# Row maxima of the attention scores from the rounded parts alone, two heads side by side in the grouped layers

## Chip, core and metric

One NeuronCore of one Trainium2 chip. The metric is the device time of one execution in microseconds (us), lower is better. The kernel before has a median of 4727.58 us over three runs (4726.94 to 4730.17).

## What is computed

Four cross-attention layers run one after the other on x (8 batches, 512 tokens, 512 channels) with one context (8 batches, 512 keys, 1024 channels). Layer 0 has 16 heads of 64 channels and a bias on four key columns; layers 1 to 3 normalise x first and have 16 query heads of 32 channels that share 4 key/value heads. Cut to what matters:

```python
# layer 0
logits = einsum('bhqd,bhkd->bhqk', x @ Wq, ctx @ Wk) * 64 ** -0.5 + col_bias
x = softmax(logits) @ (ctx @ Wv) @ Wo + bo + x
# layers 1 to 3 (n_rep = 4 query heads per key head)
xn = x * rsqrt(mean(x * x) + eps) * norm_w
scores = einsum('btgrd,bsgd->bgrts', qg, k) / sqrt(32)
x = x + softmax(scores) @ v @ wo
```

A softmax is the same whatever constant is subtracted from a row of scores before the exponential, as long as numerator and denominator use the same one. The kernel subtracts a row maximum only to keep the exponentials in range.

## The kernel before, in words

`project_context` (L42) runs twice and leaves keys and values of all layers in DRAM. `attention_layers` (L221) runs for layer 0 (no norm, d = 64, H = 2 heads in a tile of 128 channels, T = 8 tiles) and then, in one loop, for layers 1 to 3 (the grouped layers: norm, d = 32, H = 4, T = 4). The loop over `it` takes a batch of a layer: 8 rounds in layer 0, 24 in the grouped layers; inside it stand T tiles t.

Every number is split into a rounded part (hi) and a rest (lo), and a product is hi·hi + hi·lo + lo·hi. For the scores the three products are stacked along the contraction: `q_ops` holds (hi, hi, lo) and `k_ops` (hi, lo, hi) on successive groups of d partitions, `PASS` = 4d/128 matmuls per product (two in layer 0, one in the grouped layers). Partition 96 of the last pass carries minus the row maximum in `q_ops` and ones in `k_ops`, so that `scores` (L941) leaves the shifted scores in PSUM, and ScalarE takes the exponential (L699).

TensorE's order is written out by hand (L1008 to L1069). While it makes the scores of tile t (S0, S1, ... below: `scores(it, t, n)`, the product of 128 keys of two heads), it also makes the maxima of tile t + 1 (M0, M1, ...: `maxima`, L920, 128 queries by 512 keys of one head, M = 8 in layer 0 and 16 in the grouped layers), which VectorE reduces one by one (`reduce_max`, L800). M0 to M15 cycle through the PSUM banks of `MAXB` (L322), and a maximum waits until the reduction of the last user of its bank is done (L927). In a grouped tile the order before is S0 S1, M0 M1 S2, M2 S3 M3, M4 S4 M5 O0, M6 S5 M7 O1, M8 S6 M9, M10 S7 M11 O2, M12 M13, O3 M14 M15, D, the turn, P. O0 to O3 are `outputs` (L955, probabilities times values, one matmul per head in its own 32 or 64 columns of the array), D is `denominators` (L972, likewise in columns), the turn (L934) transposes the maxima, P is `project_q` (L905, 12 matmuls) for tile t + 3. In layer 0: S0, M0 S1 M1, M2 S2 M3 O0, M4 S3 M5 O1, M6 M7 O2, O3, the turn, nine matmuls of P, D, the last three of P. After the last tile of a round stands `project_out` (L983).

VectorE's order is also written out (L847 to L895). In a tile after the first one: `take_q` (L788), the rest of the reciprocals (L823) of the tile before, the reduction of M0, in layer 0 one more reciprocal and the reduction of M1, then `normalise` (L826), then the other reductions. O0 waits for `normalise` (L963), because both use one PSUM bank.

GpSimd adds up probabilities for the denominators (L593) and makes the rests (L599, L603). SyncE issues all DMAs: `load_k` (L409), `load_q` (L423, which spreads hi and lo over `q_ops`), x and results. K and Q tiles lie in rings of four (`RING`), loaded three tiles ahead (`AHEAD`). In layer 0 the x of the next round is split in two halves in tile 5 (L442, L640, L809), and P of that tile needs both.

Of the kernel before, what the change touches and what calls it, by code (L numbers as in the profile page):

```python
# [5 lines left out]
P = 128  # L6
# [214 lines left out]
def attention_layers(nc, name, kind, x_in, x_out, k_scratch, v_scratch, wq, wo, norm_w=None, bias=None):  # L221
# [41 lines left out]
    with ExitStack() as mem:  # L263
        def sb(n, shape, dt):
            return mem.enter_context(nc.sbuf_tensor(f"{name}_{n}", shape, dt))
# [105 lines left out]
        def last_use(n):  # L371

            return max(m for m in range(n) if MAXB[m] == MAXB[n])

        def k_head(h):
            return 0 if kind.shared else h

# [22 lines left out]
        def raw_chunk(c, slot):  # L400
            n = (CK if c < HALF else T) // HALF
            return w_raw[:, slot, :].rearrange("p (k n) -> p k n", k=n), range((c % HALF) * n, (c % HALF + 1) * n)

        block = mem.enter_context(nc.Block())
        X0 = P - d

        @block.sync
        def _(sp):
            def load_k(it, t, n=None):  # L409

                s = t % RING
                b, l = (0, 0) if n is None else (n % B, n // B)
                for i, part in enumerate((0, 1, 0)):
                    at = (i * d) % P
                    dst = as_f32(k_ops[at:at + d, s, :, (i * d) // P, :])
                    if kind.shared:
                        src = k_scratch[b, INNER0 // P + l, part][t * d:(t + 1) * d, :]
                        src = src.rearrange("(h p) s -> p h s", h=1)
                    else:
                        src = k_scratch[b, t, part].rearrange("(h p) s -> p h s", h=H)  # L420
                    sp.dma_start(dst, src).then_inc(k_in[s], DMA)

            def load_q(it, t):  # L423
                s = t % RING
                sp.wait_ge(q_lo, it * T + t + 1)
                for h in range(H):
                    for i, part in enumerate((qn_hi, qn_hi, qn_lo)):
                        at = (i * d) % P
                        sp.dma_start(as_f32(q_ops[at:at + d, s, h, (i * d) // P, :]),
                                     as_f32(part[h * d:(h + 1) * d, :])).then_inc(q_in[s], DMA)  # L430

            def load_v(t, n=None):
                b, l = (0, 0) if n is None else (n % B, n // B)
# [121 lines left out]
                sp.wait_ge(w_in[0], (2 * L + 2) * DMA)  # L555
                sp.wait_ge(nw_in, (L + 1) * DMA)
            for t in range(AHEAD):
                sp.wait_ge(k_in[t], ring_count(N, t) * (3 * DMA))
# [4 lines left out]
        def _(pool):  # L563
# [32 lines left out]
            def rest_q(it, t):  # L596
                if has_norm:
                    pool.wait_ge(q_hi, it * T + t + 1)
                    pool.tensor_tensor(qn_lo[:, :], qf[:, :], as_f32(qn_hi[:, :]), ALU.subtract).then_inc(q_lo, 1)  # L599

            def rest_output(it, t):
                pool.wait_ge(o_hi, it * T + t + 1)
# [21 lines left out]
        def _(act):  # L624
# [26 lines left out]
            def round_q(it, t, first=False):  # L651
                if has_norm:
                    act.wait_ge(q_taken, it * T + t + 1)
                else:
                    act.wait_ge(q_proj, it * T + t + 1)
                if not first:
                    it_p, t_p = (it, t - 1) if t > 0 else (it - 1, T - 1)
                    act.wait_ge(q_in[t_p % RING], ring_count(it_p, t_p) * (3 * H * DMA))
                if has_norm:
                    act.activation(qn_hi[:, :], qf[:, :], ACT.Copy).then_inc(q_hi, 1)  # L660
                else:
                    act.activation(qn_hi[:, :], bank(QB), ACT.Copy, scale=scale).then_inc(q_hi, 1)

            def shift(it, t):

# [62 lines left out]
        def _(dve):  # L728
# [59 lines left out]
            def take_q(it, t, first=False):  # L788
                if has_norm:
                    dve.wait_ge(q_proj, it * T + t + 1)  # L790
                    if not first:
                        dve.wait_ge(q_lo, it * T + t)
                    dve.wait_ge(inv_done, it + 1)
                    dve.tensor_tensor(qf[:, :], bank(QB), inv[:, :], ALU.mult).then_inc(q_taken, 1)
                else:
                    dve.wait_ge(q_hi, it * T + t + 1)
                    dve.scalar_tensor_tensor(out=qn_lo[:, :], in0=bank(QB), scalar=scale, in1=as_f32(qn_hi[:, :]),
                                             op0=ALU.mult, op1=ALU.subtract).then_inc(q_lo, 1)

            def reduce_max(it, t, n):  # L800
                dve.wait_ge(smax, (it * T + t) * M + n + 1)
                col = n % QT + 32 * (n // QT)
# [95 lines left out]
        def _(pe):  # L898
# [20 lines left out]

            def maxima(it, t, n):  # L920

                s = t % RING
                if n == 0:
                    pe.wait_ge(k_in[s], ring_count(it, t) * (3 * DMA))
                    pe.wait_ge(q_in[s], ring_count(it, t) * (3 * H * DMA))
                elif MAXB[n] in MAXB[:n]:
                    pe.wait_ge(reduced, (it * T + t) * M + last_use(n) + 1)  # L927
                h, q = n // QT, n % QT
# [12 lines left out]
            def scores(it, t, n):  # L941

                s, kt, hp = t % RING, n // (H // 2), n % (H // 2)
                if n == 0:
                    pe.wait_ge(shifted, it * T + t + 1)
# [62 lines left out]
            with pe.Fori(0, N) as it:  # L1008
                for t in range(T):
# [4 lines left out]
                    if t == 0 and H == 2:  # L1014
                        pe.wait_ge(added, CK + it * CK - 2)
                    for r in range(NS):
                        if has_norm and r == NS - 1:
                            outputs(it, t, KT - 1)
                        if MAXB.index(DENB) in (2 * r, 2 * r + 1):
                            pe.wait_ge(normed, 1 + it * T + t)  # L1020
                        maxima(*place(it, t + 1), 2 * r)

                        summing = has_norm and t == 0 and r == NS // 2
                        if summing:

                            pe.wait_ge(reduced, (it * T + t + 1) * M + last_use(2 * r + 1) + 1)
                            sum_squares(it + 1)
                        if t == 0 and r == 0 and H == 2:
                            pe.wait_ge(added, CK + it * CK)
                        if H // 2 + r < NS and not (r == 0 and has_norm):  # L1030
                            scores(it, t, H // 2 + r)
                        if r == 0:
                            pe.wait_ge(bank_q, it * T + t + AHEAD)
                        if not summing:
                            maxima(*place(it, t + 1), 2 * r + 1)
                        if r == 0 and has_norm:
                            scores(it, t, H // 2)
                        if r in OUT_AT and not (r == NS - 1 and has_norm):
                            outputs(it, t, OUT_AT.index(r))
                        if summing:  # L1040
                            pe.wait_ge(ms_step, MS * (it + 1) + 1)
                            maxima(*place(it, t + 1), 2 * r + 1)
                    if not has_norm:
                        outputs(it, t, KT - 1)
                    else:
# [67 lines left out]
```

## Time and profile before

| | |
|---|---|
| median of 3 runs | 4727.58 us |
| runs | 4730.17, 4727.58, 4726.94 us |
| span of the profiled execution | 4730.0 us (all but equal to the highest run, 2.4 above the median) |
| busy: PE (TensorE matmul), weight loads | 94%, 57% |
| busy: VectorE, ScalarE, GpSimd | 54%, 41%, 33% |
| stages by the span: keys, values, layer 0, grouped layers | to 580, to 1062, to 2412, to 4730 us |

A busy PE is not a PE at its peak: an entry of the profile lasts from issue to the modelled end, so neighbours overlap, and what a matmul costs in a stream is the distance between starts. The prediction reads those distances from the timeline.

### The profile page before, as it was taken

Reading aid. Unit: us, or ns where it says so; the run is one execution under the profiler, and the core shown is the slowest. Engines: PE = TensorE matmul, PEld = TensorE weight load, DVE = VectorE, ACT = ScalarE, POOL = GpSimd, SP = SyncE. Lnnn points to the kernel's source line nnn. Section 1 sums busy time; section 2 is a strip of 40 time slices with the busy share of each in tenths; the row PEclk is TensorE's granted clock in tenths of the full one; section 3 lists DMA queues with packets and bytes.
Section 4 is the critical chain, followed back from the end, with each engine's and each line's share of the span. In section 5 each row is a group of like instructions: output and inputs, shape, how many; then the busy total and the mean of one; then the engine's idle time right before and its main releaser. Section 6 shows DMA issues by size and latency. Waiting matters only on the chain. (4 is left out here: it accounts for less than half of the span.)

```text
span 4730.0 us, 63902 instructions
## 1 busy us (share of the span) xinstructions
PE 4434.4 (94%) x20450; PEld 2718.5 (57%) x20450; DVE 2572.9 (54%) x3575; ACT 1926.9 (41%) x2348; POOL 1579.5 (33%) x827
## 2 busy tenths in 40 slices
PE   7999799978999999999969999999999999999998
PEld 6888688864555655565535454445444544454454
DVE  2211200015455455544557767776777677767776
ACT  2111211113333333333326555655565555555554
POOL 0000000002444435434424444444444443444444
PEclk9999899998999999999979999999999999999999
DMA  4333422234434444444432232232222222222233
GB/s 158 127 129 133 148 83 82 80 99 120 115 100 118 115 108 111 118 107 113 113 89 71 82 88 71 75 98 83 73 74 86 84 82 75 84 85 73 75 89 95
DMA packets 301727, 461.94 MB, mean 98 GB/s; under 512 B 44954, under 2 KB 95130, under 8 KB 301692
## 3 DMA queue, kind: packets, MB, share of 16 engines
q1 hardware_dynamic: 301692, 461.50, 33.6%
q8 instruction: 19, 0.31, 0.0%
q14 instruction: 16, 0.13, 0.0%
HBM read 227.88 MB, written 102.76 MB: 70 GB/s over the span
## 5 line engine op out<-in xcount | busy, mean ns | idle before, releaser
L803 DVE TENSOR_REDUCE a_max_cols<-a_ps 128x1 f32<-128x512 f32 x2072 | 1343.8, 680 | 422.7 <-PE a_ps L930 419.3
L699 ACT ACTIVATE a_probs<-a_ps 128x1024 f32<-128x1024 f32 x1024 | 1018.6, 1026 | 730.7 <-PE a_ps L951 727.1
L930 PE MATMUL a_ps<-a_k_ops,a_q_ops 96*128 96x512 f32 (+1 forms) x2592 | 957.9, 435 | 71.9 <-DVE a_max_cols L803 50.8
L930 PEld LDWEIGHTS a_ps<-a_k_ops,a_q_ops 96*128 96x128 f32 (+1 forms) x2592 | 459.4, 190 | 696.2 <-DVE a_max_cols L803 547.3
L951 PE MATMUL a_ps<-a_q_ops,a_k_ops 128*128 128x512 f32 x2560 | 785.2, 409 | 37.7 <-ACT a_probs L699 19.1
L823 DVE RECIPROCAL a_stage<-a_ps 128x128 f32<-128x128 f32 x640 | 571.6, 928 | 396.1 <-PE a_ps L979 396.0
L593 POOL TENSOR_TENSOR a_probs<-a_probs 128x1024 f32<-128x1024 f32 x192 | 462.6, 2409 | 729.7 <-PE a_ps L967 708.5
L967 PE MATMUL a_ps<-a_probs,a_v 128*32 128x512 f32 (+1 forms) x4096 | 677.2, 612 | 0.0
L668 ACT ACTIVATE a_q_ops<-a_ps 1x512 fp32r<-1x512 f32 x518 | 304.9, 589 | 781.7 <-PE a_ps L938 777.3
L951 PEld LDWEIGHTS a_ps<-a_q_ops,a_k_ops 128*128 128x128 f32 x2560 | 463.9, 190 | 206.8 <-ACT a_probs L699 82.7
L599 POOL TENSOR_TENSOR a_qn_lo<-a_qf,a_qn_hi 128x512 fp32r<-128x512 f32 x99 | 126.5, 1278 | 1040.9 <-ACT a_qn_hi L660 1040.9
L593 POOL TENSOR_TENSOR a_sums<-a_probs 128x1024 f32<-128x1024 f32 x192 | 453.8, 2382 | 0.0
L915 PE MATMUL a_ps<-a_x_hi,a_wq_hi 128*128 128x512 f32 x664 | 289.6, 436 | 76.2 <-DVE a_x_lo L809 68.3
L569 POOL MEMSET a_ident<- 128x128 f32 x2 | 0.4, 204 | 1064.3 <-POOLq L51 1039.7
L196 PE MATMUL vp_ps<-vp_w_hi,vp_c_hi 128*128 128x512 f32 (+1 forms) x768 | 286.2, 373 | 34.9 <-DVE vp_c_lo L154 33.2
L603 POOL TENSOR_TENSOR a_a_lo<-a_stage,a_a_hi 128x512 fp32r<-128x512 f32 x160 | 213.5, 1335 | 290.2 <-ACT a_a_hi L674 290.2
L196 PE MATMUL kp_ps<-kp_c_hi,kp_w_hi 128*128 128x512 f32 x704 | 275.3, 391 | 33.3 <-DVE kp_c_lo L154 29.1
L196 PE MATMUL vp_ps<-vp_w_hi,vp_c_lo 128*128 128x512 f32 (+1 forms) x768 | 286.4, 373 | 0.0
L196 PE MATMUL vp_ps<-vp_w_lo,vp_c_hi 128*128 128x512 f32 (+1 forms) x768 | 286.2, 373 | 0.0
L154 DVE TENSOR_TENSOR vp_c_lo<-vp_raw,vp_c_hi 128x1024 fp32r<-128x1024 f32 x36 | 44.1, 1225 | 438.6 <-ACT vp_c_hi L131 438.6
L196 PE MATMUL kp_ps<-kp_c_lo,kp_w_hi 128*128 128x512 f32 x704 | 274.7, 390 | 0.0
L196 PE MATMUL kp_ps<-kp_c_hi,kp_w_lo 128*128 128x512 f32 x704 | 274.6, 390 | 0.0
(88 smaller groups left out, 5315.9 us busy)
## 6 DMA issues: line engine op xcount, KB each, us to landing
a_k_ops<-k_scratch SPq DMA_DIRECT2D x201, 256.0 KB, 3.9
a_q_ops<-a_qn_hi SPq DMA_DIRECT2D x792, 64.0 KB, 2.0
k_scratch<-kp_out SPq DMA_DIRECT2D x88, 512.0 KB, 2.8
a_q_ops<-a_qn_hi SPq DMA_DIRECT2D x268, 128.0 KB, 2.3
a_x_raw<-out_t SPq DMA_DIRECT2D x26, 1024.0 KB, 5.2
a_q_ops<-a_qn_lo SPq DMA_DIRECT2D x396, 64.0 KB, 2.0
a_x_res<-out_t SPq DMA_DIRECT2D x96, 256.0 KB, 3.1
out_t<-a_results SPq DMA_DIRECT2D x96, 256.0 KB, 2.0
```

The costliest lines, as they stand in the source:

```text
L196: last = pe.matmul(ps[:, m % 2, 0:width(n)], stationary, moving, start=(k == 0 and i == 0), stop=(k == KC - 1 and i == 2))
L593: pool.tensor_tensor(sums[:, hp], (probs if i == 1 else sums)[:, hp], probs[:, n], ALU.add)\
L599: pool.tensor_tensor(qn_lo[:, :], qf[:, :], as_f32(qn_hi[:, :]), ALU.subtract).then_inc(q_lo, 1)
L603: pool.tensor_tensor(a_lo[:, t, :], stage[:, t % 2, :], as_f32(a_hi[:, t, :]), ALU.subtract)\
L668: ins = act.activation(q_ops[SHIFT:SHIFT + 1, t % RING, h, PASS - 1, :], ps[32 * h:32 * h + 1, TURNB, :], ACT.Copy)
L699: act.activation(probs[:, s], ps[:, 2 * (s % 2):2 * (s % 2) + 2, :], ACT.Exp)\
L803: dve.tensor_reduce(max_cols[:, col:col + 1], bank(MAXB[n]), AX.X, ALU.max, negate=True).then_inc(reduced, 1)
L823: dve.reciprocal(stage[:, t % 2, i * n:(i + 1) * n], bank(DENB)[:, i * n:(i + 1) * n])\
L915: last = pe.matmul(bank(QB), w[:, k, t * P:(t + 1) * P], x[:, k, :], start=(k == 0 and i == 0), stop=(k == CK - 1 and i == 2))
L930: last = pe.matmul(bank(MAXB[n]), q_ops[0:rows(p), s, h, p, q * P:(q + 1) * P], k_ops[0:rows(p), s, k_head(h), p, :], start=(p == 0), stop ...
L951: last = pe.matmul(bank(2 * (n % 2) + j), k_ops[:, s, k_head(h), p, kt * P:(kt + 1) * P], q_ops[:, s, h, p, :], start=(p == 0), stop=(p == ...
L967: last = pe.matmul(ps[h * d:(h + 1) * d, OUTB, :], v[:, kt, c0:c0 + d], probs[:, kt * (H // 2) + h // 2, h % 2, :], start=(kt == 0), stop= ...
```

## The change

The parts of q are stacked as (lo, hi, hi) instead of (hi, hi, lo). With k still (hi, lo, hi), the last 64 channels of layer 0 (its second pass) are then hi·hi with the bias rows, and a maximum is that one matmul over 96 partitions instead of two. In the grouped layers a maximum is the product over the 32 partitions of its own head in `qn_hi` (now a ring of four) with keys on the same partitions: `k_ops` holds them at 0 and 64, a new tile `k_max` at 32 and 96, filled by two more DMAs per tile. Successive maxima take successive heads, and M(2r) and M(2r+1) are issued next to each other. The grouped order becomes S0 S1, S2 M0 M1, M2 M3 S3, M4 M5 S4 O0, M6 M7 S5 O1, M8 M9 S6, M10 M11 S7 O2, M12 M13, O3 M14 M15, D, the turn, P (in tile 0 the sum of squares stands between M8 and M9, as before). Maxima no longer wait for the q loads, scores do. The maxima are now those of the rounded product alone, in all layers; the scores keep all three products.

```diff
-        qn_hi = sb("qn_hi", [P, S], F32R)
+        qn_hi = sb("qn_hi", [P, RING if kind.shared else 1, S], F32R)
+        k_max = sb("k_max", [P, RING, S], F32R) if kind.shared else None
-        MAXB = (4, 5, 4, 5, 7, 4, 5, 7, 4, 5, 7, 4, 5, 4, 5, 4) if has_norm else (4, 5, 4, 5, 7, 4, 5, 4)
+        MAXB = (4, 5, 4, 5, 7, 4, 5, 7, 4, 5, 7, 4, 5, 7, 4, 5) if has_norm else (4, 5, 4, 5, 7, 4, 5, 4)
+        def max_place(n):
+            return (n % H, n // H) if kind.shared else (n // QT, n % QT)
...
+        KIN = 5 if kind.shared else 3
...
+                if kind.shared:
+                    for h in (1, 3):
+                        sp.dma_start(as_f32(k_max[h * d:(h + 1) * d, s, :]),
+                                     k_scratch[b, INNER0 // P + l, 0][t * d:(t + 1) * d, :]).then_inc(k_in[s], DMA)
...
-                    for i, part in enumerate((qn_hi, qn_hi, qn_lo)):
+                    hi = qn_hi[h * d:(h + 1) * d, qn_slot(t), :]
+                    for i, part in enumerate((qn_lo[h * d:(h + 1) * d, :], hi, hi)):
...
             def maxima(it, t, n):
...
-                for p in range(PASS):
-                    last = pe.matmul(bank(MAXB[n]), q_ops[0:rows(p), s, h, p, q * P:(q + 1) * P],
-                                     k_ops[0:rows(p), s, k_head(h), p, :], start=(p == 0), stop=(p == PASS - 1))
-                last.then_inc(smax, 1)
+                if kind.shared:
+                    at = slice(h * d, (h + 1) * d)
+                    keys = k_max[at, s, :] if h % 2 else k_ops[at, s, 0, 0, :]
+                    pe.matmul(bank(MAXB[n]), qn_hi[at, s, q * P:(q + 1) * P], keys,
+                              start=True, stop=True).then_inc(smax, 1)
+                else:
+                    pe.matmul(bank(MAXB[n]), q_ops[0:SHIFT, s, h, PASS - 1, q * P:(q + 1) * P],
+                              k_ops[0:SHIFT, s, h, PASS - 1, :], start=True, stop=True).then_inc(smax, 1)
...
             def denominators(it, t):
...
+                if has_norm:
+                    pe.wait_ge(reduced, (it * T + t + 1) * M + M - MAXB[::-1].index(DENB))
...
+                        if has_norm:
+                            if r == NS - 1:
+                                outputs(it, t, KT - 1)
+                            if r == 0:
+                                scores(it, t, H // 2)
+                                pe.wait_ge(bank_q, it * T + t + AHEAD)
+                            if MAXB.index(DENB) in (2 * r, 2 * r + 1):
+                                pe.wait_ge(normed, 1 + it * T + t)
+                            maxima(*place(it, t + 1), 2 * r)
...
+                                maxima(*place(it, t + 1), 2 * r + 1)
+                            if 0 < r < NS - H // 2:
+                                scores(it, t, H // 2 + r)
+                            if r in OUT_AT and r < NS - 1:
+                                outputs(it, t, OUT_AT.index(r))
...
-    nc = bacc.Bacc("TRN2", target_bir_lowering=False, num_devices=1)
+    nc = bacc.Bacc("TRN2", target_bir_lowering=False, num_devices=1, dynamic_dma_scratch_size=1024)
```

## Rows read from the trace of the kernel before

**Rows 1.** Busy time by stage: layer 0, then the grouped layers

```profile
core 0: us, PE busy (x) PEld busy (x) DVE busy (x) ACT busy (x) POOL busy (x), PEclk, DMA share, GB/s
1062.00:2412.00 1350.00, 1269.34 (x5176) 762.90 (x5176) 692.97 (x974) 445.79 (x554) 552.78 (x261) 0.97 0.43 113
2412.00:4730.00 2318.00, 2196.68 (x10858) 1134.46 (x10858) 1693.42 (x2405) 1282.03 (x1522) 1022.04 (x559) 0.98 0.28 81
```

**Rows 2.** Timeline, PE, a middle tile of layer 0: start us, us, what

```profile
1639.55 1.08 PE L951 MATMUL a_ps<-a_q_ops,a_k_ops 128*128 128x512 f32 x4
1640.46 0.62 PE L930 MATMUL a_ps<-a_k_ops,a_q_ops 128*128 128x512 f32 x2
...
1642.64 0.74 PE L930 MATMUL a_ps<-a_k_ops,a_q_ops 128*128 128x512 f32 x2 [0.17 <-DVE a_max_cols L803]
...
1644.72 1.08 PE L967 MATMUL a_ps<-a_probs,a_v 128*64 128x512 f32 x4
...
1651.79 0.66 PE L938 MATMUL a_ps<-a_ident,a_max_cols 128*128 128x128 f32 x4
...
1654.45 1.08 PE L979 MATMUL a_ps<-a_probs,a_ones 128*64 128x512 f32 x4
```

**Rows 3.** Timeline, VectorE and GpSimd, the same tile

```profile
1641.96 0.63 DVE L803 TENSOR_REDUCE a_max_cols<-a_ps 128x1 f32<-128x512 f32 x1
...
1643.90 0.67 DVE L828 TENSOR_TENSOR a_stage<-a_ps,a_stage 128x512 f32<-128x512 f32 x1
...
1645.89 2.38 POOL L593 TENSOR_TENSOR a_probs<-a_probs 128x1024 f32<-128x1024 f32 x1 [8.04 <-PE a_ps L967]
...
1651.04 2.38 POOL L593 TENSOR_TENSOR a_probs<-a_probs 128x1024 f32<-128x1024 f32 x1 [0.16 <-POOL a_probs L593]
```

**Rows 4.** Timeline, PE, tile 5 of a round of layer 0: P after its wait

```profile
1368.61 0.80 PE L915 MATMUL a_ps<-a_x_hi,a_wq_hi 128*128 128x512 f32 x1 [2.83 <-DVE a_x_lo L809]
```

**Rows 5.** Timeline, PE, tile 3 of a round of the grouped layers

```profile
2897.61 1.09 PE L951 MATMUL a_ps<-a_q_ops,a_k_ops 128*128 128x512 f32 x4
...
2899.36 0.73 PE L951 MATMUL a_ps<-a_q_ops,a_k_ops 128*128 128x512 f32 x2 [0.18 <-ACT a_probs L699]
...
2901.16 0.73 PE L930 MATMUL a_ps<-a_k_ops,a_q_ops 96*128 96x512 f32 x2 [0.15 <-DVE a_max_cols L803]
...
2902.60 1.07 PE L967 MATMUL a_ps<-a_probs,a_v 128*32 128x512 f32 x8
...
2904.41 0.40 PE L930 MATMUL a_ps<-a_k_ops,a_q_ops 96*128 96x512 f32 x1
2904.74 1.07 PE L967 MATMUL a_ps<-a_probs,a_v 128*32 128x512 f32 x8
...
2907.81 1.06 PE L967 MATMUL a_ps<-a_probs,a_v 128*32 128x512 f32 x8
...
2910.47 0.74 PE L930 MATMUL a_ps<-a_k_ops,a_q_ops 96*128 96x512 f32 x2
2911.13 1.06 PE L979 MATMUL a_ps<-a_sums,a_ones 128*32 128x512 f32 x8
...
2917.10 0.44 PE L986 MATMUL a_ps<-a_a_hi,a_wo_hi 128*128 128x512 f32 x1
```

**Rows 6.** Timeline, VectorE, the same tile

```profile
2899.28 0.63 DVE L803 TENSOR_REDUCE a_max_cols<-a_ps 128x1 f32<-128x512 f32 x1
2899.83 0.68 DVE L828 TENSOR_TENSOR a_stage<-a_ps,a_stage 128x512 f32<-128x512 f32 x1
2900.42 3.16 DVE L803 TENSOR_REDUCE a_max_cols<-a_ps 128x1 f32<-128x512 f32 x5
...
2906.27 2.59 DVE L803 TENSOR_REDUCE a_max_cols<-a_ps 128x1 f32<-128x512 f32 x4 [0.74 <-PE a_ps L930]
```

**Rows 7.** Timeline, VectorE, the first reductions in tile 0 of a grouped round

```profile
2837.64 3.98 DVE L803 TENSOR_REDUCE a_max_cols<-a_ps 128x1 f32<-128x512 f32 x6 [1.07 <-PE a_ps L930]
```

**Rows 8.** DMA issues of the grouped keys: count, KB each, us to landing

```profile
a_k_ops<-k_scratch SPq DMA_DIRECT2D x297, 64.0 KB, 1.8
```

More of the change, by code:

```diff
@@ L373, in last_use, with qn_slot @@
             return max(m for m in range(n) if MAXB[m] == MAXB[n])
+        def max_place(n):
+            return (n % H, n // H) if kind.shared else (n // QT, n % QT)
+        def qn_slot(t):
+            return t % RING if kind.shared else 0
         def k_head(h):
@@ L426, in load_q @@
                 for h in range(H):
-                    for i, part in enumerate((qn_hi, qn_hi, qn_lo)):
+                    hi = qn_hi[h * d:(h + 1) * d, qn_slot(t), :]
+                    for i, part in enumerate((qn_lo[h * d:(h + 1) * d, :], hi, hi)):
                         at = (i * d) % P
                         sp.dma_start(as_f32(q_ops[at:at + d, s, h, (i * d) // P, :]),
-                                     as_f32(part[h * d:(h + 1) * d, :])).then_inc(q_in[s], DMA)
+                                     as_f32(part)).then_inc(q_in[s], DMA)
             def load_v(t, n=None):
@@ L557, in _ @@
             for t in range(AHEAD):
-                sp.wait_ge(k_in[t], ring_count(N, t) * (3 * DMA))
+                sp.wait_ge(k_in[t], ring_count(N, t) * (KIN * DMA))
                 sp.wait_ge(q_in[t], ring_count(N, t) * (3 * H * DMA))
@@ L598, in rest_q @@
                     pool.wait_ge(q_hi, it * T + t + 1)
-                    pool.tensor_tensor(qn_lo[:, :], qf[:, :], as_f32(qn_hi[:, :]), ALU.subtract).then_inc(q_lo, 1)
+                    pool.tensor_tensor(qn_lo[:, :], qf[:, :], as_f32(qn_hi[:, qn_slot(t), :]), ALU.subtract).then_inc(q_lo, 1)
             def rest_output(it, t):
@@ L659, in round_q @@
                 if has_norm:
-                    act.activation(qn_hi[:, :], qf[:, :], ACT.Copy).then_inc(q_hi, 1)
+                    act.activation(qn_hi[:, qn_slot(t), :], qf[:, :], ACT.Copy).then_inc(q_hi, 1)
                 else:
-                    act.activation(qn_hi[:, :], bank(QB), ACT.Copy, scale=scale).then_inc(q_hi, 1)
+                    act.activation(qn_hi[:, qn_slot(t), :], bank(QB), ACT.Copy, scale=scale).then_inc(q_hi, 1)
             def shift(it, t):
@@ L796, in take_q @@
                     dve.wait_ge(q_hi, it * T + t + 1)
-                    dve.scalar_tensor_tensor(out=qn_lo[:, :], in0=bank(QB), scalar=scale, in1=as_f32(qn_hi[:, :]),
+                    dve.scalar_tensor_tensor(out=qn_lo[:, :], in0=bank(QB), scalar=scale, in1=as_f32(qn_hi[:, qn_slot(t), :]),
                                              op0=ALU.mult, op1=ALU.subtract).then_inc(q_lo, 1)
@@ L801, in reduce_max @@
                 dve.wait_ge(smax, (it * T + t) * M + n + 1)
-                col = n % QT + 32 * (n // QT)
+                h, q = max_place(n)
+                col = q + 32 * h
                 dve.tensor_reduce(max_cols[:, col:col + 1], bank(MAXB[n]),
@@ L922, in maxima @@
                 s = t % RING
+                h, q = max_place(n)
                 if n == 0:
-                    pe.wait_ge(k_in[s], ring_count(it, t) * (3 * DMA))
-                    pe.wait_ge(q_in[s], ring_count(it, t) * (3 * H * DMA))
+                    pe.wait_ge(k_in[s], ring_count(it, t) * (KIN * DMA))
+                    if kind.shared:
+                        pe.wait_ge(q_hi, it * T + t + 1)
+                    else:
+                        pe.wait_ge(q_in[s], ring_count(it, t) * (3 * H * DMA))
                 elif MAXB[n] in MAXB[:n]:
                     pe.wait_ge(reduced, (it * T + t) * M + last_use(n) + 1)
-                h, q = n // QT, n % QT
-                for p in range(PASS):
-                    last = pe.matmul(bank(MAXB[n]), q_ops[0:rows(p), s, h, p, q * P:(q + 1) * P],
-                                     k_ops[0:rows(p), s, k_head(h), p, :], start=(p == 0), stop=(p == PASS - 1))
-                last.then_inc(smax, 1)
+                if kind.shared:
+                    at = slice(h * d, (h + 1) * d)
+                    keys = k_max[at, s, :] if h % 2 else k_ops[at, s, 0, 0, :]
+                    pe.matmul(bank(MAXB[n]), qn_hi[at, s, q * P:(q + 1) * P], keys,
+                              start=True, stop=True).then_inc(smax, 1)
+                else:
+                    pe.matmul(bank(MAXB[n]), q_ops[0:SHIFT, s, h, PASS - 1, q * P:(q + 1) * P],
+                              k_ops[0:SHIFT, s, h, PASS - 1, :], start=True, stop=True).then_inc(smax, 1)
             def turn(it, t):
@@ L944, in scores @@
                 if n == 0:
+                    if kind.shared:
+                        pe.wait_ge(q_in[s], ring_count(it, t) * (3 * H * DMA))
                     pe.wait_ge(shifted, it * T + t + 1)
@@ L1016, in _ @@
                     for r in range(NS):
[L1017 to L1021, printed above, removed]
-                        summing = has_norm and t == 0 and r == NS // 2
-                        if summing:
-                            pe.wait_ge(reduced, (it * T + t + 1) * M + last_use(2 * r + 1) + 1)
-                            sum_squares(it + 1)
@@ L1028, in _ @@
[L1028 to L1034, printed above, removed]
-                            maxima(*place(it, t + 1), 2 * r + 1)
-                        if r == 0 and has_norm:
-                            scores(it, t, H // 2)
@@ L1038, in _ @@
[L1038 to L1042, printed above, removed]
+                        summing = has_norm and t == 0 and r == NS // 2
+                        if has_norm:
[7 more added lines that the diff above has]
+                            maxima(*place(it, t + 1), 2 * r)
+                            if summing:
+                                pe.wait_ge(reduced, (it * T + t + 1) * M + last_use(2 * r + 1) + 1)
+                                sum_squares(it + 1)
+                            else:
+                                maxima(*place(it, t + 1), 2 * r + 1)
[3 more added lines that the diff above has]
+                                outputs(it, t, OUT_AT.index(r))
+                            if summing:
+                                pe.wait_ge(ms_step, MS * (it + 1) + 1)
+                                maxima(*place(it, t + 1), 2 * r + 1)
+                        else:
+                            if MAXB.index(DENB) in (2 * r, 2 * r + 1):
+                                pe.wait_ge(normed, 1 + it * T + t)
+                            maxima(*place(it, t + 1), 2 * r)
+                            if t == 0 and r == 0 and H == 2:
+                                pe.wait_ge(added, CK + it * CK)
+                            if H // 2 + r < NS:
+                                scores(it, t, H // 2 + r)
+                            if r == 0:
+                                pe.wait_ge(bank_q, it * T + t + AHEAD)
+                            maxima(*place(it, t + 1), 2 * r + 1)
+                            if r in OUT_AT:
+                                outputs(it, t, OUT_AT.index(r))
```

## The prediction, made before the changed kernel was run

> **What bounds the kernel now.** I read the busy time by stage first. In both stages that the change touches PE is busy 94 to 95% of the time, at a granted clock of 0.97 to 0.98 of 2.4 GHz, and VectorE 51% (layer 0) and 73% (grouped) [rows 1]. An average hides where one engine waits for the other inside a tile, so the rest comes from the timeline of one tile per stage. Keys and values (to 1062 us) do not change.
>
> Costs of PE by distances between starts: S0 and M0 stand 0.91 apart with four matmuls, 0.23 us each [rows 2]; M11 to O1 is 0.33, a pair of maxima between two blocks in columns 0.66 instead of 0.46 [rows 5]. So entering the column arrangement costs 0.10, and after leaving it the first full matmul costs about 0.11 more; O0 to the next maximum is 1.00 for two passes of four matmuls side by side, some 0.1 of it the leaving. Matmuls over 96 and over 128 partitions follow each other without any such cost.
>
> **Layer 0.** 520 second matmuls of maxima disappear (64 tiles of 8 and 8 at the start), 0.23 each: 119 us if PE alone decided. It doesn't. In a middle tile, from S0 at 1639.55: M2 waits already (0.17) for the reduction of M0, which VectorE starts at 1641.96 after work that hangs on the end of P, not on M0 [rows 2, 3]. O0 at 1644.72 needs `normalise`, which starts at 1643.90 and takes 0.67 [rows 3]. With one matmul per maximum PE reaches M2 0.46 and M3 0.7 earlier and waits that long: O0 comes at 1644.6, 0.1 earlier. From O0 to D four maxima (M4 to M7) shrink by 0.23 each, 0.92. Their cover is GpSimd's three sums, from 1645.89 to 1653.42 [rows 3], 1.0 ahead of D at 1654.45 [rows 2]; they hang on O0 and move with it by 0.1, so D may come 1.05 earlier at most, and 1.02 is taken. Middle tile: -1.0. Six tiles of a round are like that. Tile 0 has its `normalise` behind it and keeps most of 8 x 0.23 = 1.84: -1.6. In tile 5 P waits 2.83 for the second half of x [rows 4], a chain of DMA, ScalarE and VectorE that hangs on M3's reduction: PE arrives earlier and waits longer, 0. Per round -7.7, eight rounds: **-62 us**. Bounds: -119 (all of it on the path), and -30 (the sums or the x chain take half of it back). I take -62, since each of its limits has a row.
>
> The new order of parts in `q_ops` moves no DMA: each already waits for the lo part.
>
> **Grouped layers, the price of a pair.** 97 x 16 maxima become 776 pairs. Side by side a pair costs one stream, 0.23 instead of 0.46, as the four heads of an output do, which take 1.00 together [rows 5]: 8 x 0.23 = 1.84 per tile. But maxima over 32 partitions use the array in another arrangement than the full matmuls around them. No row shows a change between full and row arrangement. Its nearest row is that between full and columns: 0.10 to let the array run empty, and 0.11 for a weight load that nothing hides. The other bound is that of 96 to 128 partitions: nothing. Before, a tile has five column blocks, ten changes. After, I count 18 in the new order: eight more, up to 0.21 each, 1.7. On PE alone the gain is gone. I take the column price, as both are changes of the array's tiles.
>
> The Trainium skill, page "TensorEngine Tiling (Array Packing)", section "Tiling Modes", says that changing the tiling mode, as against changing the tile within one, makes the engine drain, and it lists row modes beside column modes. By this rule the sum is the one of my forecast; without it, that of the second case below. The trace agrees for columns (0.33 against 0.23); nothing run so far shows it for rows.
>
> **Grouped layers, the chain.** Positions in a middle tile, from S0 = 0 at 2897.61 to the end of P at 19.49 [rows 5].
> - S0 to M3. Before: M0 at 0.93, its reduction at 1.67 (2899.28), `normalise` at 2.22, M1's reduction at 2.81 [rows 6], M3 at 3.55. After: S2 goes first, and it waits for the first exponential until 1.75 [rows 5]; S2 ends at 2.21, M0 at 2.31, its reduction 0.53 later (O1 at 2904.74 ends its slot of 1.00 at 2905.74, where the next maximum starts; VectorE, idle for 0.74, begins with it at 2906.27 [rows 5, 6]). Reduction of M0 at 2.84, `normalise` 3.4, M1's reduction 4.0, done 4.6. M2 and M3 need banks 4 and 5 and so these two reductions: M3 at 4.66, and this pair never runs side by side. **+1.1**.
> - M3 to O0: S3 (0.46) now stands here, and three changes of arrangement (0.21 each), against two maxima less and a stall of 0.15. Before 1.44, after 2.11: **+0.67**.
> - O0 to O1: a pair saves 0.23, a change costs 0.21: **0**.
> - O1 to O2: M8/M9 save 0.23; M11 needs bank 4 and waits for M8's reduction; two more S between row blocks: **+0.13**.
> - O2 to the end: M12/M13 and M14/M15 between column blocks, each pair 0.66 before and 0.44 after: **-0.46**. A new wait stands before D, for M13's reduction, since M13 now uses D's bank; D and behind it the turn and P are queued there. M12 starts at 13.1, so VectorE is done with M13 at 14.8 (0.53, then two reductions of 0.62); D starts at 14.93 and loses nothing.
> Sum +1.4. VectorE's idle time before M6 to M15 (0.74 and its like) shrinks, and I find no further wait. Tile 0 has no `normalise` and no reciprocals in front of its maxima (six reductions in a row [rows 7]) and M9 waits for the mean square in either order: +0.5. Tiles 1 and 2 I take like the middle one: their extra work (x split, a table load) lies on VectorE and ScalarE and delays P or the first exponential in either order. Per round 3 x 1.4 + 0.5 = 4.7, 24 rounds: **+113 us**.
>
> Edits that I cost at nothing. Two more key DMAs of 64 KB per tile: the present ones land in 1.8 [rows 8] and are used two tiles later; on SyncE they are queued behind nothing that is late, and stand ahead of `load_q`, which waits for the lo part of q anyway; if that cover were gone, it would be their issue, about 1.3 per tile. The wait for q moved from maxima to scores comes a tile later than before, so it relaxes. The ring of `qn_hi` adds no wait. The smaller scratch for dynamic DMAs has nothing to hold here: all DMAs are issued by SyncE.
>
> **Sum.** The profiled span is 4730.0; -62 + 113 gives 4781. The median of the runs lies 2.4 below the span: **4778 us**, 1.1% slower.
>
> **Rivals.**
> 1. *Changes between full and row arrangement are free.* Then the same chain: M3 at 4.55 (+1.0, it hangs on reductions), to O0 +0.07, to O1 -0.23, to O2 -0.04, to the end -0.49: +0.3 in a middle tile, -0.5 in tile 0, +0.4 per round, +10 in all. 4730 - 62 + 10 - 2 = **4676**, faster. For it: 96 to 128 partitions costs nothing. Against: the column rows.
> 2. *The array runs empty, but the weight load stays hidden*: 0.10 for each of the eight changes. A middle tile then loses 1.05, tile 0 comes out even: 3.2 per round, +76, **4742**, 0.3% slower.
> 3. *The weight loads of a pair run one after the other*: the second maximum starts 0.11 late in about five unwaited pairs per tile, 0.5 x 96 = 48 on top of the forecast: **4826**.
> 4. *PE's saving comes out whole*: 119 + 776 x 0.22 = 290 less, **4438**. For it: PE is the busiest engine in both stages [rows 1], and the average alone would promise this. Against it: the stall of M2 in layer 0 and VectorE's run of reductions without idle time after `normalise` in the grouped tile, 5 in 3.16 [rows 2, 3, 6]; nobody shortens those.
>
> The other side of my forecast is rival 1; the point from which it decides is the price of a change of arrangement. The grouped layers lose 10 at a price of nothing and 76 at 0.10 (rival 2), so below some 0.08 us they lose less than the 62 that layer 0 gains.
>
> **How the numbers follow.** Forecast 0.46, rival 1 0.29, rival 2 0.13, rival 3 0.07, rival 4 0.05. A measurement of this kernel can tell 0.2% (9.5 us) from no change. Slower: forecast and rival 3 (0.53) and a third of rival 2 (0.04), 0.57; the rest of rival 2 is within 0.2%, 0.09; faster: rivals 1 and 4, 0.34. Each case has some 35 us of its own, from the limits of layer 0 and 0.3 per grouped tile in my placing of waits; the forecast's own range is 4740 to 4815. The range reaches down to rival 1, 4665, and up to 4815; left out are rival 4 and most of rival 3.
>
> **What would show it.** Right: in layer 0's middle tiles D 14.9 after S0 before [rows 2] and about 13.9 after the change, tile 5 as long as before; D right behind the third sum; M2 waiting 0.6 for VectorE. In the grouped layers middle tiles of 20.9; the last full matmul before a row pair with a slot of 0.33, the first one after it 0.34; two maxima of a pair some nanoseconds apart except M2 and M3. Wrong: if full and row matmuls follow each other at 0.23 (rival 1), if the second of a pair starts 0.11 or more after the first (rival 3), or if S2 no longer holds back M0.

## The result, and the profile after

The changed kernel takes 5106.4 us (5088.97 to 5113.39, four runs) against 4727.75: a ratio of 1.0794, 95% interval 1.0775 to 1.0813. Slower was forecast, but by 50 us, and it is 379; the value lies far outside the stated range of 4665 to 4815.

The busy time by stage of the changed kernel (compare [rows 1]), from the last turn (the transposes of the maxima) of layer 0 to the end of the span, as in all tables below:

```profile
core 0: us, PE busy (x) PEld busy (x) DVE busy (x) ACT busy (x) POOL busy (x), PEclk, DMA share, GB/s
2308.00:5107.70 2799.70, 2526.02 (x10976) 1109.73 (x10974) 1700.58 (x2419) 1316.09 (x1532) 1023.90 (x566) 0.85 0.26 74
```

and the same stretch of the kernel before:

```profile
2365.00:4730.00 2365.00, 2223.41 (x10976) 1155.17 (x10974) 1711.00 (x2419) 1291.18 (x1532) 1029.74 (x566) 0.98 0.28 82
```

The number that matters stands behind the busy times: the granted clock of TensorE (PEclk, 1.00 is 2.4 GHz), 0.98 before, 0.85 after. The number of PE's instructions is the same (10976). Layer 0, from its first turn to its last, went from 1261.1 to 1204.4 us, -57; the grouped stage from 2365 to 2800, +435. The page of the profile shows it in one line. It cuts the span into 40 slices; the grouped layers start in the 19th, which stands at 7 tenths, and of the 21 after it 18 stand at 8:

```profile
PEclk9999899979999999997888888888888989888898
```

In the records of the clock, which know two levels, PE is at 1.2 GHz for 771 us of this stage in 101 stretches, against 55 us in 8 before. Both are counted from the second turn of the stage on; its first tile has some 40 us more in every kernel of this study, before the change too.

**Layer 0**, a middle tile (compare [rows 2, 3]), PE from D to D:

```profile
1611.27 1.08 PE L1010 MATMUL a_ps<-a_probs,a_ones 128*64 128x512 f32 x4
...
1613.10 1.09 PE L980 MATMUL a_ps<-a_q_ops,a_k_ops 128*128 128x512 f32 x4
1614.02 0.40 PE L958 MATMUL a_ps<-a_k_ops,a_q_ops 96*128 96x512 f32 x1
...
1616.17 0.50 PE L958 MATMUL a_ps<-a_k_ops,a_q_ops 96*128 96x512 f32 x1 [0.57 <-DVE a_max_cols L822]
...
1618.21 1.08 PE L996 MATMUL a_ps<-a_probs,a_v 128*64 128x512 f32 x4
...
1624.35 0.66 PE L965 MATMUL a_ps<-a_ident,a_max_cols 128*128 128x128 f32 x4
...
1627.01 1.08 PE L1010 MATMUL a_ps<-a_probs,a_ones 128*64 128x512 f32 x4
```

One matmul for M0; M2 comes 3.07 after S0 as before (3.09) and now waits 0.57 for VectorE; O0 stands 5.11 after S0 (5.17 before); from O0 to the turn it is 6.14 instead of 7.07. D of the next tile starts at 1627.01, 13.91 after S0 (13.9 forecast) and 0.1 after GpSimd's third sum, which ends at 1626.91. The tile is 15.8 us instead of 16.7.

**A grouped tile** (tile 2 of a round), PE from S0 on (compare [rows 5]):

```profile
3365.94 1.07 PE L980 MATMUL a_ps<-a_q_ops,a_k_ops 128*128 128x512 f32 x4
...
3367.67 0.73 PE L980 MATMUL a_ps<-a_q_ops,a_k_ops 128*128 128x512 f32 x2 [0.66 <-ACT a_probs L717]
3368.34 0.50 PE L955 MATMUL a_ps<-a_k_ops,a_qn_hi 32*128 32x512 f32 x1
3368.34 0.49 PE L955 MATMUL a_ps<-a_k_max,a_qn_hi 32*128 32x512 f32 x1
...
3369.62 0.50 PE L955 MATMUL a_ps<-a_k_ops,a_qn_hi 32*128 32x512 f32 x1 [0.79 <-DVE a_max_cols L822]
...
3370.81 0.50 PE L955 MATMUL a_ps<-a_k_max,a_qn_hi 32*128 32x512 f32 x1 [0.70 <-DVE a_max_cols L822]
...
3371.24 0.74 PE L980 MATMUL a_ps<-a_q_ops,a_k_ops 128*128 128x512 f32 x2
...
3372.34 1.22 PE L980 MATMUL a_ps<-a_q_ops,a_k_ops 128*128 128x512 f32 x2
...
3373.49 1.94 PE L996 MATMUL a_ps<-a_probs,a_v 128*32 128x512 f32 x8
```

Up to S3 (3371.24) this is the forecast in form: S2 held back by the first exponential, two maxima starting together, M2 and M3 apart, each behind a reduction, M3 4.87 after S0 (4.66 forecast, 3.55 before). Half of the missing 0.2 is S2: its two matmuls take 0.67 after the wait, where 0.56 was worked out. A row pair takes 0.43 from M3 to S3, arrangement change and all. Then comes what was not forecast: S4 (3372.34) takes 1.15 instead of 0.67, and the eight matmuls of O0, 1.00 before, take 1.87. They run at half the clock. The window view of the same tile, three stretches, shows it in the granted clock (1.00, 0.57, 1.00):

```profile
3362.00:3372.00 10.00, 7.49 (x32) 4.58 (x30) 8.07 (x11) 7.00 (x9) 2.87 (x2) 1.00 0.03 7
3372.00:3376.00 4.00, 4.00 (x15) 1.11 (x15) 1.32 (x3) 2.56 (x3) 3.60 (x3) 0.57 0.40 98
3376.00:3386.00 10.00, 10.00 (x65) 3.33 (x63) 6.67 (x11) 3.07 (x3) 3.03 (x2) 1.00 0.54 170
```

What PE did just before it fell: four full matmuls, a wait of 0.66, S2, a pair of row maxima, a wait of 0.79, one row maximum, a wait of 0.70, one more. None of these waits is as long as those of 2.83 in layer 0 [rows 4]; in the whole stage the longest wait of a maximum for a reduction is 1.7.

### The profile page after: what moved, and what is told of

The parts are those of the page before. It is cut to its first block, busy times and chain, and to the rows that moved or that the text cites. A ratio compares the mean times of both kernels' runs of the same rounds, so it can differ in the third digit from the quotient of the medians.

```text
span 5107.7 us, 63444 instructions
## 1 busy us (share of the span) xinstructions
PE 4638.8 (91%) x19930; PEld 2579.4 (51%) x19930; DVE 2560.9 (50%) x3575; ACT 1951.1 (38%) x2348; POOL 1574.6 (31%) x827
## 4 chain that ended last, share of the span: by engine, by line
issue 27%; PE 15%; POOL 8%; DVE 3%; ACT 2%; SPq 0%; POOLq 0%; DVEq 0%; ACTq 0%; DMA 0%
POOL a_sums L611 4%; PE a_ps L1017 3%; PE a_ps L980 3%; POOL a_a_lo L621 2%; PE a_ps L955 2%; PE a_ps L996 2%; ACT a_probs L717 1%; PE a_ps L934 1%; PE a_ps L1010 1%; DVE a_max_cols L822 1%; POOL a_qn_lo L617 1%; PE a_ps L922 1%; ACT a_x_hi L658 0%; DVE a_ms L804 0%; DVE a_stage L847 0%
## 5 line engine op out<-in xcount | busy, mean ns | idle before, releaser
L717 ACT ACTIVATE a_probs<-a_ps 128x1024 f32<-128x1024 f32 x1024 | 1039.6, 1023 | 1177.4 <-PE a_ps L980 1168.7
L980 PE MATMUL a_ps<-a_q_ops,a_k_ops 128*128 128x512 f32 x2560 | 925.9, 467 | 65.1 <-ACT a_probs L717 50.0
L996 PE MATMUL a_ps<-a_probs,a_v 128*32 128x512 f32 (+1 forms) x4096 | 817.1, 756 | 7.8
L955 PE MATMUL a_ps<-a_k_ops,a_qn_hi 32*128 32x512 f32 x776 | 446.4, 575 | 79.8 <-DVE a_max_cols L822 79.8
L955 PEld LDWEIGHTS a_ps<-a_k_ops,a_qn_hi 32*128 32x128 f32 x776 | 163.3, 210 | 688.3 <-issue 360.6
L955 PE MATMUL a_ps<-a_k_max,a_qn_hi 32*128 32x512 f32 x776 | 441.3, 579 | 64.0 <-DVE a_max_cols L822 48.0
```

The costliest lines, as they stand in the source:

```text
L717: act.activation(probs[:, s], ps[:, 2 * (s % 2):2 * (s % 2) + 2, :], ACT.Exp)\
L955: pe.matmul(bank(MAXB[n]), qn_hi[at, s, q * P:(q + 1) * P], keys, start=True, stop=True).then_inc(smax, 1)
L996: last = pe.matmul(ps[h * d:(h + 1) * d, OUTB, :], v[:, kt, c0:c0 + d], probs[:, kt * (H // 2) + h // 2, h % 2, :], start=(kt == 0), stop= ...
```

## The experiments

All ratios are to the kernel before on the same chip. "Half" is the time at 1.2 GHz in the grouped stage by the clock records, from its second turn on. "M waits" is the time in us that the maxima of the stage wait for reductions, all added up. A "full" tile is the distance of two turns (the transposes) with none of it in between, median, for tiles 0, 1, 2, 3 of a round.

| run | median us | ratio, 95% interval | grouped stage | half | M waits | full tiles |
|---|---|---|---|---|---|---|
| before | 4727.8 | | 2365 | 55 | 40 | 33.4, 20.1, 20.0, 19.5 |
| changed | 5106.4 | 1.0794 (1.0775 to 1.0813) | 2800 | 771 | 128 | none |
| e1_layer0_only | 4673.5 | 0.9886 (0.9869 to 0.9902) | 2363 | 50 | 42 | 33.3, 20.1, 20.0, 19.5 |
| e2_order_full | 4838.6 | 1.0235 (1.0218 to 1.0252) | 2526 | 180 | 109 | 33.7, 21.2, 21.6, 21.2 |
| e3_rows_old_order | 4794.4 | 1.0145 (1.0128 to 1.0162) | 2481 | 141 | 20 | 34.5, 20.6, 21.0, 20.6 |
| e4_keepers | 4881.0 | 1.0322 (1.0304 to 1.0339) | 2572 | 199 | 2 | 34.6, 21.4, 22.0, 21.4 |
| e5_maxima_first | 4798.3 | 1.0143 (1.0115 to 1.0170) | 2499 | 307 | 65 | 33.7, 20.0, 20.6, 20.0 |
| f1_one_row_group | 5329.3 | 1.1287 (1.1262 to 1.1312) | 3012 | 1004 | 108 | none |
| g1_keep_row | 5092.7 | 1.0747 (1.0704 to 1.0790) | 2793 | 754 | 56 | 34.3 (three of tile 0), 21.4 (two of tile 3) |
| g2_keep_full | 4868.9 | 1.0295 (1.0277 to 1.0313) | 2567 | 184 | 2 | 34.8, 21.4, 22.0, 21.4 |
| e6_hybrid | 4624.6 | 0.9779 (0.9762 to 0.9795) | 2315 | 51 | 19 | 32.9, 19.3, 19.7, 19.1 |
| h2_hybrid_o01 | 4593.8 | 0.9716 (0.9700 to 0.9733) | 2285 | 56 | 19 | 32.6, 19.1, 19.4, 18.7 |

**e1_layer0_only**, on the kernel before:

```diff
-                    for i, part in enumerate((qn_hi, qn_hi, qn_lo)):
+                    for i, part in enumerate((qn_lo, qn_hi, qn_hi)):
...
-                for p in range(PASS):
-                    last = pe.matmul(bank(MAXB[n]), q_ops[0:rows(p), s, h, p, q * P:(q + 1) * P],
-                                     k_ops[0:rows(p), s, k_head(h), p, :], start=(p == 0), stop=(p == PASS - 1))
+                pe.matmul(bank(MAXB[n]), q_ops[0:SHIFT, s, h, PASS - 1, q * P:(q + 1) * P],
+                          k_ops[0:SHIFT, s, k_head(h), PASS - 1, :], start=True, stop=True).then_inc(smax, 1)
```

> The layer 0 part of the change alone: q stacked as (lo, hi, hi), one matmul per maximum in layer 0, the grouped layers exactly as before. Both theories: layer 0 takes 1204 us from its first to its last turn as in the changed kernel (1261 before), the grouped layers 2365 us as before, in all 4728 - 57 = 4671. If layer 0's shorter tiles carried anything over into the grouped layers, the second number would differ.

Measured 4673.5, layer 0 1204.8, grouped stage as before (2363 for 2365). The layer 0 part is worth its -57 by itself and carries nothing over. All that the changed kernel loses, it loses in the grouped layers.

**e2_order_full**, on the changed kernel (cut to the matmul; the first maximum of a tile also waits for the q loads again, as before the change):

```diff
-                    pe.matmul(bank(MAXB[n]), qn_hi[at, s, q * P:(q + 1) * P], keys,
-                              start=True, stop=True).then_inc(smax, 1)
+                    pe.matmul(bank(MAXB[n]), q_ops[0:SHIFT, s, h, 0, q * P:(q + 1) * P],
+                              k_ops[0:SHIFT, s, 0, 0, :], start=True, stop=True).then_inc(smax, 1)
```

> The changed kernel with its new order and banks in the grouped layers, but every maximum over 96 partitions of the full array (all three products, as before); no row arrangement. Theory A (the new order leaves PE with little work between S2 and S3 and that brings the clock down): the clock still falls, time below 1.2 GHz steps in hundreds of us, 4900 or more. Theory B (matmuls over 32 partitions bring the clock down): clock as before, chain alone +1.1 in a middle tile and about 4755 in all.

Between the two: 4838.6, and 180 us at half speed. Its full tiles sum to 4.7 more per round than before: the new order costs 113 us of the 161 without any row maximum, the clock the rest. Theory A says too much, B too little: the order lets the clock fall in 41 stretches, but 590 us of the 771 need the row maxima as well. The waits themselves are nearly those of the changed kernel, 109 us against 128.

**e3_rows_old_order**, on the changed kernel, TensorE's loop and banks of before:

```diff
-        MAXB = (4, 5, 4, 5, 7, 4, 5, 7, 4, 5, 7, 4, 5, 7, 4, 5) if has_norm else (4, 5, 4, 5, 7, 4, 5, 4)
+        MAXB = (4, 5, 4, 5, 7, 4, 5, 7, 4, 5, 7, 4, 5, 4, 5, 4) if has_norm else (4, 5, 4, 5, 7, 4, 5, 4)
...
                             maxima(*place(it, t + 1), 2 * r)
...
                             if H // 2 + r < NS and not (r == 0 and has_norm):
                                 scores(it, t, H // 2 + r)
...
                             maxima(*place(it, t + 1), 2 * r + 1)
```

> The changed kernel's maxima over 32 partitions, but with the order and the banks of before in the grouped layers (M0 M1 S2, M2 S3 M3, ...). 23 changes of arrangement per tile instead of 18, and five pairs side by side. Chain alone: +1.6 per tile, 4671 + 150 = 4820. Theory A: the waits at the start of a tile are those of before, few falls of the clock, 4800 to 4850. Theory B: the clock falls as in the changed kernel, 5000 or more.

4794.4, 141 us at half speed, in 13 stretches: near theory A, 6 us below its range and 26 below the 4820 of the chain. Thirteen more changes of arrangement and five pairs come to +1.1, +0.5, +1.0 and +1.1 in the full tiles, where 1.6 each was worked out; some of the changes lie under waits. Row maxima without the long waits (20 us of them in all) cost 86 us more at half speed than before the change, not 716.

**e4_keepers**, on the changed kernel; `keep(3)` before M2, `keep(5)` before M3:

```diff
+            def keep(it, t, count):
+                pe.wait_ge(exped, (it * T + t) * NS + 2)
+                s = (t + 1) % RING
+                for _ in range(count):
+                    for h in range(2):
+                        at = slice(h * d, (h + 1) * d)
+                        keys = k_max[at, s, :] if h % 2 else k_ops[at, s, 0, 0, :]
+                        pe.matmul(bank(2 + h), qn_hi[at, s, 0:P], keys, start=True, stop=True)
```

> The changed kernel with extra work: while PE would wait for the reductions of M0 and M1, it makes 3 and 5 more pairs of row matmuls into the two score banks that S3 overwrites next (16 matmuls more per grouped tile, results unused). Theory A: the clock falls less often (half speed in well under 500 us of the 754 measured), the time drops below 5000 although more is computed. Theory B: no drop, 5106 or a little more.

With 16 matmuls more per tile, whose results nobody reads, the kernel is 225 us faster than the changed one. M3 starts 4.87 after S0, the same; only the waits are filled. Half speed falls from 771 to 199 us (the expectation has 754 for the 771), and the waits of the maxima from 128 to 2. That is the clean evidence for the clock: nothing was taken away from the work, and M0 to M3 start where they did. The grouped stage:

```profile
2307.00:4878.60 2571.60, 2413.47 (x12510) 1171.37 (x12508) 1702.28 (x2419) 1314.92 (x1532) 1029.59 (x566) 0.95 0.28 80
```

**e5_maxima_first**, on the changed kernel (order S0 S1, M0 M1 S2, S3 M2 M3, M4 M5 S4 O0, ...):

```diff
                             if r == 0:
-                                scores(it, t, H // 2)
                                 pe.wait_ge(bank_q, it * T + t + AHEAD)
+                            if r == 1:
+                                scores(it, t, H // 2 + r)
...
-                            if 0 < r < NS - H // 2:
+                            if r == 0 or 1 < r < NS - H // 2:
                                 scores(it, t, H // 2 + r)
```

> The changed kernel with M0 M1 issued before S2 again and S3 before M2 M3; row maxima, pairs and banks unchanged. If the late first maxima are the cause: M3 about 3.5 us after S0 instead of 4.9, the two long waits gone, few falls of the clock (under 150 us at half speed instead of 771), middle tile 19.7 to 20.3, in all 4690 to 4750. If the row maxima alone keep the clock low: still above 4950.

M3 comes 3.5 after S0 as forecast, and the full tiles are 20.0, 20.6 and 20.0 (forecast 19.7 to 20.3). The total is 48 us above the upper end, for the clock is still down for 307 us in 33 stretches. The forecast that the long waits go was half right: before M2 and M3 PE stands idle no longer, but M5 now waits 0.54 to 0.56 for its bank, and the waits of the maxima add up to 65 us, half of the changed kernel's:

```profile
3358.10 0.50 PE L955 MATMUL a_ps<-a_k_max,a_qn_hi 32*128 32x512 f32 x1 [0.54 <-DVE a_max_cols L822]
```

The order of the first maxima accounts for 464 of the 771 us at half speed.

**f1_one_row_group**, on the changed kernel:

```diff
-            return (n % H, n // H) if kind.shared else (n // QT, n % QT)
+            return n // QT, n % QT
```

> The changed kernel with the heads in the old sequence, so that successive maxima lie on the same 32 partitions and can't run side by side; everything else as changed. Each pair takes 0.23 more: at full clock +1.2 per grouped tile on the changed kernel. If the clock follows the time in which PE streams: less time at half speed than 771 us, in all 4950 to 5100, faster than the changed kernel although it streams longer. If matmuls over 32 partitions count too little whatever their time: as many falls, 5200 or more.

5329.3 and 1004 us at half speed in 100 stretches, as many as in the changed kernel: PE streams the maxima for twice as long and the clock is no better. The same order with the same number of maxima one after the other, but over 96 partitions, is e2_order_full with 180 us, and the maxima wait as long in both (108 and 109 us). It doesn't separate everything: in the row form the array also changes its arrangement 18 times per tile, in the other 10 times.

**g1_keep_row** and **g2_keep_full**, the changed kernel with the waits filled for the same time, by row matmuls (`keep(2)` and `keep(2)` of e4_keepers) or by full ones (`keep(1)` and `keep(1)` of this form):

```diff
+                s = t % RING
+                for h in range(2 * count):
+                    pe.matmul(bank(2 + h), k_ops[:, s, 0, 0, P:2 * P], q_ops[:, s, h, 0, :], start=True, stop=True)
```

> The changed kernel with extra row matmuls in the two waits again, but 2 and 2 pairs (8 matmuls per grouped tile, two streams of 0.23 in each wait) instead of 3 and 5. If the clock follows what PE does in this stretch: between the changed kernel (5106) and e4_keepers (4881), less than 771 us at half speed and more than 199, about 4950 to 5050.

> The same waits filled with 2 and 2 matmuls over the full array (128 partitions, into the score banks that S3 overwrites), so the same time of streaming as g1_keep_row, two streams of 0.23 in each wait, plus up to four changes of arrangement per tile that fit into the waits. If only the time in which PE streams matters: as g1_keep_row. If matmuls over more partitions count for more: less time at half speed than in g1_keep_row and a shorter run, 4880 to 4950.

The grouped stage of g1_keep_row, then of g2_keep_full:

```profile
2306.00:5098.90 2792.90, 2590.57 (x11744) 1149.82 (x11742) 1700.89 (x2419) 1316.94 (x1532) 1025.48 (x567) 0.86 0.26 74
```

```profile
2306.00:4873.80 2567.80, 2402.34 (x11362) 1117.07 (x11358) 1701.97 (x2419) 1314.25 (x1532) 1028.63 (x567) 0.96 0.28 80
```

Two streams of 0.23 in each wait: over 128 partitions the clock stays (0.96, 184 us at half), over 32 and 32 side by side it hardly changes (0.86, 754 us). So g1_keep_row missed its expectation (4950 to 5050) on the slow side, and g2_keep_full is 11 us below its range. This pair does not show, though, that a matmul over more partitions does more for the clock, because the waits are not equally full. With its changes of arrangement the full pair covers the whole wait (2 us of waits are left in the stage); the row pairs leave 56 us, in one tile 0.30 before M2 and 0.46 before M3:

```profile
3387.58 0.50 PE L955 MATMUL a_ps<-a_k_ops,a_qn_hi 32*128 32x512 f32 x1 [0.30 <-DVE a_max_cols L822]
...
3388.77 0.50 PE L955 MATMUL a_ps<-a_k_max,a_qn_hi 32*128 32x512 f32 x1 [0.46 <-DVE a_max_cols L822]
```

In e4_keepers, where eight row pairs leave 2 us of waits, the clock is down for 199 us, nearly as in g2_keep_full. That the kind of matmul counts rests on f1_one_row_group against e2_order_full, with the reservation made there.

**e6_hybrid**, the loop of before, the banks of the change, row pairs only where column blocks stand on both sides (cut to the maxima; the loop is that of e3_rows_old_order, and the first maximum of a tile waits for the q loads again):

```diff
+            def full(n):
+                return n < 12
...
+                if kind.shared and full(n):
+                    pe.matmul(bank(MAXB[n]), q_ops[0:SHIFT, s, h, 0, q * P:(q + 1) * P],
+                              k_ops[0:SHIFT, s, 0, 0, :], start=True, stop=True).then_inc(smax, 1)
```

> Order of before in the grouped layers, banks of the change; maxima over the full array for M0 to M11 and row pairs only for M12 to M15, which stand between column blocks, so that no change of arrangement is added. Layer 0 as changed. Each of the two pairs 0.44 instead of 0.66: -0.45 per tile, 96 tiles: 4673 - 43 = 4630. Clock as before. If pairs between column blocks did not pay either: 4673 or more.

4624.6, on the forecast. PE around O2, M12 M13 and O3 (before [rows 5], the pair between two column blocks took 0.66):

```profile
3008.01 1.07 PE L999 MATMUL a_ps<-a_probs,a_v 128*32 128x512 f32 x8
3009.01 0.50 PE L958 MATMUL a_ps<-a_k_ops,a_qn_hi 32*128 32x512 f32 x1
3009.01 0.50 PE L958 MATMUL a_ps<-a_k_max,a_qn_hi 32*128 32x512 f32 x1
3009.44 1.07 PE L999 MATMUL a_ps<-a_probs,a_v 128*32 128x512 f32 x8
```

It takes 0.43 now. Here a pair adds no change of arrangement, and the saving is whole.

**h2_hybrid_o01**, on e6_hybrid:

```diff
-                        if r in OUT_AT and not (r == NS - 1 and has_norm):
+                        if has_norm and r == OUT_AT[1]:
+                            outputs(it, t, 0)
+                        if r in OUT_AT and not (r in (OUT_AT[0], NS - 1) and has_norm):
```

> As e6_hybrid, with O0 moved behind M7 next to O1, so that one column block of a tile and its two changes (0.3) fall away. Chain: 0.3 less per tile, 4630 - 29 = 4600, if VectorE, which gets M6 to M8 at other times, has no longer wait in it; if it has, 4630 or more.

4593.8, again as worked out: 2.8% below the kernel before, 513 us below the changed one, and the fastest version of this study. It was not taken apart whether all of its 31 us come from the two changes. Its grouped stage keeps the clock at 0.98:

```profile
2307.00:4592.20 2285.20, 2145.33 (x10974) 1138.95 (x10974) 1689.69 (x2419) 1281.77 (x1532) 1029.70 (x566) 0.98 0.32 90
```

## Why the prediction was wrong

**Layer 0** (-62 forecast, -57 measured): right in mechanism and size. M2's wait is 0.57 (0.6), O0 comes 5.11 after S0 (5.17 before), a middle tile is 0.9 shorter (1.0 forecast), and D stands right behind the third sum. Tile 5, forecast at 0, is a little longer: median 22.1 after (21.4 to 22.5) for 21.4 before.

**The price of a pair**: right. The last full matmul before a row maximum takes 0.33 and the first one after a pair 0.34, instead of 0.23; two maxima start 3 to 4 ns apart, and a pair with the change behind it takes 0.43. The forecast weighed the rule of the Trainium skill, page "TensorEngine Tiling (Array Packing)", section "Tiling Modes", that changing the tiling mode makes the engine drain. The trace agrees with it for rows too (0.33 against 0.23). Rivals 1, 2 and 3 fall with these slots, rival 4 with the total.

**The chain**: right in form, a little short in size. The full tiles of e4_keepers, where the chain is that of the change, are +1.2, +1.3, +2.0, +1.9 on those of before, 6.4 per round or 154 us, against 4.7 and 113. The filling may carry a part of it, but g2_keep_full, filled in another way, has the same tiles within 0.2. The changed kernel has no full tile; a straight line through the lengths of its 91 inner tiles against their time at half speed, with a constant for each of the four places in a round, gives an estimate: +1.0, +1.4, +2.0, +1.7 at full clock, 144 us in all, and 0.43 us lost per us at half speed. M3 comes 0.2 later than worked out, and in tile 2 P waits 0.37 for x after a shorter lead. +0.5 for tile 0 is the most undersized, +1.2 measured.

**The step that failed** is one that was put at nothing without a reason, the cost of the clock. Every term was priced at the clock of before, "at a granted clock of 0.97 to 0.98", as if that were a property of the stage. The forecast placed M2 and M3 behind two reductions and wrote down that PE would stand there, took out half of the streaming of the maxima and put each of them on a quarter of the array's rows, and never asked what that does to the clock. The grouped stage lost 435; 154 is the chain, and the other 281 us is the clock. A second count agrees: between the changed kernel and e4_keepers 572 us less at half speed bring 225 us, 0.39 per us; at that rate the changed kernel's 716 more than before are worth 282. Both counts use e4_keepers. The line through the changed kernel's own tiles does not: it gives 144 for the chain and 0.43 x 716 = 309 for the clock, 453 for the 435 measured. So the clock took 280 to 310 us, and the chain about 150.

What makes it fall is the two together, the waits and the row maxima. The order alone (e2) gives 180 us at half speed, row maxima alone (e3) 141, both 771; filling the waits completely takes it to 184 with full matmuls and to 199 with row matmuls, filling them in part leaves 754. Which of the changed kernel's waits matters most was not taken apart. The 307 us of e5_maxima_first go with one wait per tile that stayed, but no run was made to show that it is the reason. Whether row maxima weigh less because they are over fewer partitions or because the array changes its arrangement around them is open as well.

## What to carry to other kernels

When a change makes TensorE wait more often or replaces full matmuls by ones over few partitions, look at the granted clock before the chain: here three waits of 0.7 to 0.8 us, which the chain had priced in, were followed by a stretch in which everything took nearly twice as long. Row tiles side by side pay where they stand between blocks that are in tiles already (0.43 instead of 0.66 here) and lose where full matmuls stand on both sides (two full ones and a pair 1.10, four full ones in a row 0.92). If a wait of TensorE can't be avoided, useless matmuls that fill it to the end can be cheaper than the silence (4869 or 4881 instead of 5106 us here, while a filling in part brought no more than 14 us); better is an order that has no such wait.

## What was unexpected of the hardware

- The clock fell without any long idle time: the waits before the fall were 0.66, 0.79 and 0.70 us, with matmuls between them, and no wait of a maximum in the stage was longer than 1.7.
- With equal waits and equally many maxima one after the other, those over 32 partitions let the clock down for 1004 us (f1_one_row_group), those over 96 for 180 (e2_order_full); the changes of arrangement differ too.
- Cutting the waits by more than half with four row pairs per tile hardly moved the clock (g1_keep_row: 0.86), closing them with eight did (e4_keepers: 0.95).
- At half speed the eight matmuls of an output took 1.87 instead of 1.00 us and two full ones with a change behind them 1.15 instead of 0.67.
